# Tokens and attention of a decoder block's first phase turned by VectorE through memory instead of by TensorE

## The chip, the cores and the metric

One core of one Trainium2 chip. The time of a kernel is the device time of one launch in microseconds (us), the median of several launches; lower is better.

## The reference

x and the context are 16 sequences of 512 tokens of 512 channels, fp32. Three residual blocks follow each other, each on the layer norm of x:

```python
# block 1: linear attention of 16 heads of 32, and a convolution over 3 tokens
q, k, v = split_heads(x @ Wq.T), split_heads(x @ Wk.T), split_heads(x @ Wv.T)
q, k = elu(q) + 1, elu(k) + 1
att = (q @ sum_n(k v)) / max(q @ sum_n(k), 1e-6)
x = x + (att + conv3(x)) @ Wp.T + bp
# block 2: cross attention on the context, 4 query heads of 128, one key and value head, rotary, masked softmax
# block 3: a recurrence over the 16 sequences, then a head
f, i, g = sigmoid(x @ wf.T + c @ uf.T + bf), sigmoid(...), tanh(...)
c = f * c + i * g
x = x + tanh(x @ wo.T + c_final @ uo.T + bo)
```

## The kernel before

Four phases a, b, c and d run behind each other in one program, with a queue per engine; an item is one sequence (512 tokens as T=4 tiles of 128, 512 channels as C=4 chunks of 128). Every fp32 matrix is split into a high and a low part (fp32r), and a product is three matmuls (high by high, low by high, high by low; `product`, L130 to L132). ScalarE (ACT) copies the high part, VectorE (DVE) subtracts it for the low part.

Phase a (`phase_a`) is a pipeline of two stages over B=16 items. Step s works on item new=s (keys, values, queries, the state k v) and on old=s-1 (attention, output projection). The order on TensorE (PE) in a step is written out by hand in `step` under `tensor`: four times `attend(t)` of old (L861) and the key product of new, then four value products with `turn_att(c)` (L870) behind each, four query products, the k v sums (L927), the turning of the next item's tokens with `turn_x` (L363; three chunks, the fourth inside the output), and four tiles of the output projection of old. A product is 12 matmuls of 512 columns. `turn_x` and `turn_att` are TensorE transposes of 128x128 blocks by the identity into PSUM, four for each chunk: the products need tokens and attention with the channels on the partitions, and layer norm and attention leave them with the tokens there.

DVE in a step (`vector`): the division of the attention in six groups (`attend`, L702 to L709), `elu_back` of the keys (L695), the norm of the next item (statistics L333, the scale by a power on GpSimd (POOL) L351, `norm_apply` L357), then `z_sum` = turned attention plus convolution (L762) and its low part (L756), `elu_back` of the queries, the mask of k v (L781), the low part of the next tokens (`tokens_low`, L806), the residual (L670) and the two outer taps of the convolution (`outer_taps`, L811, L814). ACT does `elu_front` (L576, L578), the copies of values (L585) and of z's high part (L593), then `tokens_high` (L647) and the middle tap (L652). POOL adds the bias to the residual rows (L555). The DMA queue of SyncE (SP) stores the result of old to DRAM (L534), loads x of new+1 (L456) and the residual rows of old (L516).

The PSUM banks go round: `first` (5 banks) holds the key, value, query, k v products and turned tokens, `second` (3 banks) the attention, turned attention and output. `Rota.freed` names the event that a bank waits for.

After the last step of phase a, stage old of item 15 runs together with the first work of phase b (`self.b_turn_memory`, `keys_values`, `a_last_output`, then `turn_x` of phase b). Phase b's `b_normalise` stands on DVE behind `z_sum` and its low parts.

Phase c is the recurrence: 12 gate tiles (24 products) for each item, and 12 products for item 0. Its tokens are already turned by DVE from item 1 on: 16 DMAs (`shuffle`, L376) copy 32-partition quarters between SBUF tiles, so that each quarter of the channels lies on its own 32 partitions; `turn_squares` (L382) then transposes 32x32 squares for a chunk of 512 tokens in one instruction. Item 0 is turned by PE (`c_turn`). The turned tokens are also stored for phase d.

The core of what changes, before:

```python
for c in range(C):                       # values and the turning of the attention, PE
    if new: ...                          # product of tile c into bank V + c
    if old: turn_att(c)
...
dve.wait_ge(attT_ps.sem, attT_ps.upto(old.b, c))
dve.tensor_tensor(z_sum[c % 2][:, :], second.bank(s, TURNED + c)[:, :], local[old.par][:, c, :], ALU.add)
```

## Time and profile before

| what | us |
|---|---|
| median of 3 runs | 3132.19 (3131.71 to 3132.31) |
| the profiled execution's own time | 3132.6 |
| its span | 3130.9 |
| TensorE busy | 3089.7 |
| VectorE busy | 1834.5 |
| ScalarE busy | 1273.0 |
| GpSimd busy | 838.0 |

How to read it: the span is from the first to the last instruction. "Busy" of an engine is the time in which at least one of its instructions runs; matmuls overlap each other, so the distance between two starts, not the duration, is what one costs. An "x4" row merges four instructions that follow each other, and its duration is that of the four. In the order of time a bracket says how long the engine stood idle before the instruction, and what released it. SPq rows are DMA issues; "to landing" is from the issue to the end of the transfer. PEclk is the granted TensorE clock, as a share of 2.4 GHz.

### The profile page before, as it was taken

To read this page: it belongs to the slowest core of one execution; us is meant where nothing else is said; L and a number is where in the kernel's file an instruction comes from. 1 tells how busy PE (TensorE), PEld (TensorE's weight loads), DVE (VectorE), ACT (ScalarE), POOL (GpSimd) and SP (SyncE) were. 2 spreads that over 40 slices of the span, in tenths; PEclk is the share of its full clock that TensorE was granted. 3 is DMA by queue.
4 is the path that set the end of the run, shared out by engine and by line. 5 is a ranking of instruction groups with operands and counts; after the bars stand their busy time and mean duration, and the time that the engine had idled before them with its cause. 6 is when DMAs were issued, how large, how long until landed. Compare 5 with 4: busy or idle time off the path is not lost.

```text
span 3130.9 us, 40897 instructions
## 1 busy us (share of the span) xinstructions
PE 3089.7 (99%) x15588; PEld 2606.5 (83%) x15588; DVE 1834.5 (59%) x3961; ACT 1273.0 (41%) x2415; POOL 838.0 (27%) x699
## 2 busy tenths in 40 slices
PE   8999999999999999999999999999999999999999
PEld 7888888888878888888888877888888888888887
DVE  6667675666587877787788766423323333231355
ACT  4333333333356766666676653211112111121243
POOL 0101010110146666676666650000000000000144
PEclk9999999999999999999999999999999999999999
DMA  3121121212231221221212132211211112110386
GB/s 111 41 69 54 41 81 41 81 41 83 79 104 69 69 70 56 96 70 56 83 68 70 55 121 81 81 41 41 54 54 55 41 41 54 54 45 26 129 288 227
DMA packets 153363, 236.49 MB, mean 76 GB/s; under 512 B 11345, under 2 KB 48209, under 8 KB 153169
## 3 DMA queue, kind: packets, MB, share of 16 engines
...
## 4 chain that ended last, share of the span: by engine, by line
PE 95%; DVE 2%; issue 1%; ACT 1%; DMA 1%; SPq 0%; POOL 0%; DVEq 0%; ACTq 0%
PE c_p L130 11%; PE c_p L131 11%; PE c_p L132 11%; PE a_p L130 6%; PE a_p L132 6%; PE a_p L131 6%; PE b_n L132 5%; PE b_n L130 5%; PE b_n L131 5%; PE b_t L1622 3%; PE d_p L130 2%; PE d_p L131 2%; PE d_p L132 2%; PE a_r L130 2%; PE a_r L132 2%; PE a_p L927 2%
## 5 line engine op out<-in xcount | busy, mean ns | idle before, releaser
L1242 POOL TENSOR_SCALAR b_soft<-b_soft,b_one_in_sum 128x512 f32<-128x512 f32 x256 | 401.2, 1569 | 300.7 <-DVE b_one_in_sum L1425 300.7
L1867 ACT ACTIVATE c_gate<-c_p,c_bias 128x512 f32<-128x512 f32 x180 | 123.9, 690 | 693.1 <-PE c_p L132 693.1
L1903 DVE TENSOR_TENSOR c_gate<-c_gate,c_gate 128x512 f32<-128x512 f32 x64 | 44.2, 691 | 486.2 <-ACT c_gate L1867 486.2
L1444 DVE TENSOR_TENSOR b_p_lo<-b_t,b_p_hi 128x512 fp32r<-128x512 f32 x256 | 175.3, 685 | 159.9 <-ACT b_p_hi L1299 157.2
L1290 ACT ACTIVATE b_soft<-b_soft,b_minus_top 128x512 f32<-128x512 f32 x256 | 185.2, 724 | 180.8 <-DVE b_minus_top L1436 176.2
L351 POOL TENSOR_TENSOR kept_scale<-c_ln_ve,minus_half 128x4 f32<-128x4 f32 x16 | 16.1, 1009 | 879.6 <-DVE c_ln_ve L343 879.6
L576 ACT ACTIVATE a_elu<-a_p 128x512 f32<-128x512 f32 x128 | 76.5, 598 | 353.1 <-PE a_p L132 353.1
L351 POOL TENSOR_TENSOR a_ln_sc<-a_ln_ve,minus_half 128x4 f32<-128x4 f32 x16 | 16.3, 1017 | 694.7 <-DVE a_ln_ve L343 694.7
L1299 ACT ACTIVATE b_p_hi<-b_t 128x512 fp32r<-128x512 f32 x256 | 151.6, 592 | 108.6 <-PE b_t L1622 108.6
L1436 DVE CUSTOM_DVE_ANT_0 b_soft<-b_l,b_mask_row 128x512 f32<-128x512 f32 x256 | 175.3, 685 | 0.0
L1622 PE MATMUL b_t<-ident,b_soft 128*128 128x128 f32 x1024 | 155.3, 274 | 10.4 <-DVE b_p_lo L1444 9.2
L2090 POOL TENSOR_TENSOR d_x<-d_x,d_y 128x512 f32<-128x512 f32 x60 | 79.8, 1332 | 259.1 <-ACT d_y L2107 259.1
L1622 PEld LDWEIGHTS b_t<-ident,b_soft 128*128 128x128 f32 x1024 | 122.5, 141 | 29.6 <-DVE b_p_lo L1444 14.8
L130 PE MATMUL b_l<-b_k_hi,b_q_hi 128*128 128x512 f32 x256 | 122.7, 479 | 0.0
L695 DVE SCALAR_TENSOR_TENSOR a_q<-a_p,a_elu 128x512 f32<-128x512 f32 x64 | 44.2, 691 | 131.8 <-ACT a_elu L578 131.8
L1905 DVE TENSOR_TENSOR c_gate<-c_gate,c_c_f 128x512 f32<-128x512 f32 x64 | 44.3, 692 | 119.7 <-ACT c_gate L1867 119.7
L130 PE MATMUL c_p<-c_nT_hi,c_wi_hi 128*128 128x512 f32 x256 | 100.9, 394 | 5.3 <-ACT c_gate L1867 5.3
L130 PE MATMUL a_p<-a_Wk_hi,a_xT_hi 128*128 128x512 f32 x256 | 105.3, 411 | 0.2 <-DVE a_Wk_lo L194 0.2
L555 POOL TENSOR_TENSOR a_res<-a_res,a_bp 128x512 f32<-128x512 f32 x64 | 89.6, 1430 | 59.0 <-DMA a_res<-in_x 59.0
L130 PE MATMUL a_p<-a_Wv_hi,a_xT_hi 128*128 128x512 f32 x256 | 104.1, 407 | 0.0
L130 PE MATMUL a_r<-a_Wp_hi,a_z_hi 128*128 128x512 f32 x256 | 102.9, 402 | 0.0
L132 PE MATMUL b_l<-b_k_hi,b_q_lo 128*128 128x512 f32 x256 | 101.5, 397 | 0.0
...
## 6 DMA issues: line engine op xcount, KB each, us to landing
a_res<-in_x SPq DMA_DIRECT2D x16, 1024.0 KB, 5.8
x<-a_res SPq DMA_DIRECT2D x16, 1024.0 KB, 5.2
b_mem<-in_ctx SPq DMA_DIRECT2D x16, 1024.0 KB, 5.4
b_x<-x SPq DMA_DIRECT2D x16, 1024.0 KB, 5.5
b_res<-x SPq DMA_DIRECT2D x16, 1024.0 KB, 5.6
x<-b_res SPq DMA_DIRECT2D x16, 1024.0 KB, 4.4
c_x<-x SPq DMA_DIRECT2D x16, 1024.0 KB, 5.5
d_x<-x SPq DMA_DIRECT2D x16, 1024.0 KB, 5.6
```

Source lines behind the costliest of these rows:

```text
L130: pe.matmul(out, stationary.high, moving.high, start=first, stop=False)
L131: pe.matmul(out, stationary.high, moving.low, start=False, stop=False)
L132: return pe.matmul(out, stationary.low, moving.high, start=False, stop=last)
L555: pool.tensor_tensor(res[:, t, :], res[:, t, :], bp[:, :], ALU.add).then_inc(res_bp.sem, res_bp.unit)
L1242: pool.tensor_scalar(soft[:, at, :], soft[:, at, :], one_in_sum[:, at:at + 1], None, ALU.mult).then_inc(p_norm.sem, p_norm.unit)
L1290: act.activation(soft[:, at, :], soft[:, at, :], ACT.Exp, bias=minus_top[:, at:at + 1], scale=-1.0, accum_out=row_sum[:, at:at + 1]).then_ ...
L1299: act.activation(p[h % 2].high[:, :, t * P:(t + 1) * P], pT_bank[:, :].rearrange("p (i s) -> p i s", i=T), ACT.Copy).then_inc(p_hi.sem, p_ ...
L1436: dve.tensor_tensor_reduce(out=soft[:, at, :], in0=logit_banks[j % 2][:, :], in1=mask_row[b % 2][:, :], scale=-1.0, scalar=3e38, op0=ALU.a ...
L1444: dve.tensor_tensor(part.low, pT_bank[:, :].rearrange("p (i s) -> p i s", i=T), part.high_f32(), ALU.subtract).then_inc(p_lo.sem, p_lo.unit)
L1622: mm = pe.transpose(pT_bank[:, i * P:(i + 1) * P], soft[:, tile(old.b, j), i * P:(i + 1) * P], self.ident[:, :])
L1867: act.activation(gate[j % 2][i][:, :], gating.banks[(3 * j + i) % 6][:, :], ACT.Tanh if g == "c" else ACT.Sigmoid, bias=added[:, i, j:j + ...
L2090: pool.tensor_tensor(x[old.par][:, t, :], x[old.par][:, t, :], y[:, t % 2, :], ALU.add).then_inc(out_sb.sem, out_sb.unit)
```

## The change

Phase a: PE turns only item 0's tokens. For every later item the normed tokens are stored to DRAM (`self.out`, which is overwritten at the end), loaded back by four DMAs (`load_shuffled`) so that channel quarter q lies on partitions 32q to 32q+31, and turned by four DVE transposes (`turn_squares`) into an SBUF tile `turned_f`. The attention goes the same way, through `self.x2`, in two stores and four loads (`shuffle_att`), and four DVE transposes into `z_sum`. Turned this way, partition p of chunk c holds channel 4p+c; so the weights of phase a are turned with `spread` for all four, the convolution's parameters are loaded in that order, and item 0 uses `turn_interleaved`. Readers of the turned tokens (high part, middle tap, low part, outer taps) now read SBUF. On SP the new work stands behind the residual load, first the attention of old, then the tokens of new+1; phase b's first loads move behind it in the last step, and its output weight one step later. POOL's bias additions wait until the next item's tokens are normed. Some tiles move to other addresses.

Phase c: item 1 is turned by PE too (`c_turn` at the gate tiles 8 and 9 of item 0), with ACT copying the turned chunk out of PSUM; the DVE turning of later items moves from the start of a step to behind the second gate column.

The diff, its core (parameters, order and memory lines with no more in them than said above are left out):

```diff
@@ -376,6 +376,12 @@
+    def load_shuffled(self, sp, to, dram, b, event):
+        for q in range(4):
+            sp.dma_start(to[32 * q:32 * (q + 1), :, :].rearrange("m t (r n) -> m (t r) n", n=P),
+                         dram[b, :, q * P:(q + 1) * P].rearrange("(a m) n -> m a n", m=32)).then_inc(event.sem, event.unit)
@@ -430,9 +436,13 @@
+x_shuffled = sb("x_shuffled", [P, T, D])
+turned_f = Place(nc, self.base + 1024 * 196).tile("a_turned_f", [P, C, S])
+att_shuffled = Place(nc, self.base + 1024 * 184).tile("a_att_shuffled", [P, T, D])
...
+self.place = Place(nc, self.base + 1024 * 166)
@@ -440,20 +450,42 @@
+            shuffled, squared = ev("shuffled", 4, 16), ev("squared", C)
+            x_out, att_out = ev("x_out", 1, 16), ev("att_out", 2, 16)
...
-            att_ps, rden_sb, att_sb, attT_ps = ev("att_ps", GROUPS), ev("rden_sb", 2 * GROUPS), ev("att_sb", GROUPS), ev("attT_ps", C)
+            att_ps, rden_sb, att_sb = ev("att_ps", GROUPS), ev("rden_sb", 2 * GROUPS), ev("att_sb", GROUPS)
+            att_moved, attT = ev("att_moved", 4, 16), ev("attT", C)
...
+                if b == 1:
+                    sp.wait_ge(xT_ps.sem, xT_ps.upto(0))
+                if b >= 2:
+                    sp.wait_ge(x_out.sem, x_out.upto(b - 2))
+                sp.dma_start(x[:, :, :], self.token_rows(io["x"], b)).then_inc(N.loaded.sem, N.loaded.unit)
+            def shuffle(sp, b):
+                sp.wait_ge(N.normed.sem, N.normed.upto(b))
+                sp.dma_start(self.token_rows(self.out, b), x[:, :, :]).then_inc(x_out.sem, x_out.unit)
+                sp.wait_ge(x_out.sem, x_out.upto(b - 1))
+                if b >= 2:
+                    sp.wait_ge(squared.sem, squared.upto(b - 2))
+                self.load_shuffled(sp, x_shuffled, self.out, b, shuffled)
+            def shuffle_att(sp, b):
+                for i, (group, tiles) in enumerate(((3, slice(0, 3)), (GROUPS - 1, slice(3, T)))):
+                    sp.wait_ge(att_sb.sem, att_sb.upto(b, group))
+                    sp.dma_start(self.token_rows(self.x2, b)[:, tiles, :], att[:, tiles, :]).then_inc(att_out.sem, att_out.unit)
+                sp.wait_ge(att_out.sem, att_out.upto(b))
                 if b >= 1:
-                    sp.wait_ge(xT_ps.sem, xT_ps.upto(b - 1))
-                sp.dma_start(x[:, :, :], self.token_rows(io["x"], b)).then_inc(N.loaded.sem, N.loaded.unit)
+                    sp.wait_ge(attT.sem, attT.upto(b - 1))
+                self.load_shuffled(sp, att_shuffled, self.x2, b, att_moved)
@@ -490,16 +522,17 @@
-raw = Loader(nc, ctx, "aw", [(io[f"L0_attn_{n}"], w[n]) for n in ("Wk", "Wv", "Wq", "Wp")], (k, res, local[1], raw_p), C, self.ident, 3)
+raw = Loader(nc, ctx, "aw", [(io[f"L0_attn_{n}"], w[n]) for n in ("Wk", "Wv", "Wq", "Wp")], (k, res, local[1], raw_p), C, self.ident, 3, spread=(0, 1, 2, 3))
...
-             + [(kv_sb, g, 0) for g in range(2)] + [(tap2, c, -1) for c in range(C)], B)
-K, V, Q, KV, TURN = 0, T, 2 * T, 2 * T + C, 2 + 2 * T + C
+             + [(kv_sb, g, 0) for g in range(2)], B)
+K, V, Q, KV = 0, T, 2 * T, 2 * T + C
+start_bank = lambda c: first.banks[c + 1]
...
-              [(att_sb, g, 1) for g in range(GROUPS)] + [(z_f, c, 1) for c in range(C)] + [(x1_sb, t, 1) for t in range(T)], B)
-ATT, TURNED, OUT = 0, GROUPS, GROUPS + C
+              [(att_sb, g, 1) for g in range(GROUPS)] + [(x1_sb, t, 1) for t in range(T)], B)
+ATT, OUT = 0, GROUPS
@@ -514,12 +547,17 @@
-if new and new.b == B - 2:
+if old:
+    shuffle_att(sp, old.b)
+if following(new, B):
+    shuffle(sp, new.b + 1)
+if new and new.b == B - 1:
+    sp.wait_ge(shuffled.sem, shuffled.upto(B - 2))
+    self.b_load_mem(sp, 0)
+    sp.wait_ge(tap2.sem, tap2.upto(B - 1))
+    self.b_load_scale(sp)
+    sp.wait_ge(squared.sem, squared.upto(B - 2))
     self.b_load_output_weight(sp)
-if new and new.b == B - 1:
-    sp.wait_ge(xT_ps.sem, xT_ps.upto(B - 1))
-    self.b_load_mem(sp, 0)
-    self.b_load_scale(sp)
@@ -550,6 +588,8 @@
+if following(new, B):
+    pool.wait_ge(N.normed.sem, N.normed.upto(new.b + 1))
@@ -641,15 +681,18 @@
-act.wait_ge(xT_ps.sem, xT_ps.upto(b, c))
+if b == 0:
+    act.wait_ge(xT_ps.sem, xT_ps.upto(0, c))
+else:
+    act.wait_ge(squared.sem, squared.upto(b - 1, c))
...
-act.activation(xT.high[:, c, :], first.bank(b - 1, TURN + c)[:, :], ACT.Copy).then_inc(xT_hi.sem, xT_hi.unit)
+act.activation(xT.high[:, c, :], turned(b, c), ACT.Copy).then_inc(xT_hi.sem, xT_hi.unit)
...
-if b < 2:
+if b == 0:
     act.wait_ge(xT_lo.sem, xT_lo.upto(b, c))
-act.activation(local[b % 2][:, c, :], first.bank(b - 1, TURN + c)[:, :], ACT.Identity,
+act.activation(local[b % 2][:, c, :], turned(b, c), ACT.Identity,
@@ -664,6 +707,9 @@
+def turned(b, c):
+    return start_bank(c)[:, :] if b == 0 else turned_f[:, c, :]
@@ -754,12 +800,15 @@
+dve.wait_ge(att_moved.sem, att_moved.upto(old.b))
 for c in range(C):
-    dve.wait_ge(attT_ps.sem, attT_ps.upto(old.b, c))
-    dve.wait_ge(tap2.sem, tap2.upto(old.b, c))
...
-    dve.tensor_tensor(z_sum[c % 2][:, :], second.bank(s, TURNED + c)[:, :], local[old.par][:, c, :], ALU.add).then_inc(z_f.sem, z_f.unit)
+    squares = att_shuffled[:, :, :].rearrange("p t (n c) -> p c (t n)", c=C)[:, c]
+    dve.transpose(z_sum[c % 2][:, :], squares).then_inc(attT.sem, attT.unit)
+    dve.wait_ge(attT.sem, attT.upto(old.b, c))
+    dve.wait_ge(tap2.sem, tap2.upto(old.b, c))
+    dve.tensor_tensor(z_sum[c % 2][:, :], z_sum[c % 2][:, :], local[old.par][:, c, :], ALU.add).then_inc(z_f.sem, z_f.unit)
@@ -767,6 +816,10 @@
+if after and c == 2:
+    dve.wait_ge(shuffled.sem, shuffled.upto(after - 1))
+    for i in range(C):
+        self.turn_squares(dve, turned_f, x_shuffled, i).then_inc(squared.sem, squared.unit)
@@ -801,17 +854,16 @@
-copied = xT_hi if b < 2 else tap1
-dve.wait_ge(copied.sem, copied.upto(b, c))
-dve.tensor_tensor(xT.low[:, c, :], first.bank(b - 1, TURN + c)[:, :], xT[:, c, :].high_f32(), ALU.subtract).then_inc(xT_lo.sem, xT_lo.unit)
+dve.wait_ge(xT_hi.sem, xT_hi.upto(b, c))
+dve.tensor_tensor(xT.low[:, c, :], turned(b, c), xT[:, c, :].high_f32(), ALU.subtract).then_inc(xT_lo.sem, xT_lo.unit)
...
-bank, loc = first.bank(b - 1, TURN + c), local[b % 2]
-dve.scalar_tensor_tensor(out=loc[:, c, 1:S], in0=bank[:, 0:S - 1], scalar=conv_w[:, c, 0:1],
+row, loc = turned(b, c), local[b % 2]
+dve.scalar_tensor_tensor(out=loc[:, c, 1:S], in0=row[:, 0:S - 1], scalar=conv_w[:, c, 0:1],
...
-dve.scalar_tensor_tensor(out=loc[:, c, 0:S - 1], in0=bank[:, 1:S], scalar=conv_w[:, c, 2:3],
+dve.scalar_tensor_tensor(out=loc[:, c, 0:S - 1], in0=row[:, 1:S], scalar=conv_w[:, c, 2:3],
@@ -881,6 +926,8 @@
+if s == 0 and t >= 1:
+    pe.wait_ge(tap2.sem, tap2.upto(0, t - 1))
@@ -927,28 +974,21 @@
-                    if following(new, B):
-                        for c in range(C - 1 if old else C):
-                            turn_x(new.b + 1, c)
...
-                            if following(new, B) and t == 0:
-                                turn_x(new.b + 1, C - 1)
-
-                def turn_x(b, c):
+                def first_turn(c):
                     if c == 0:
-                        pe.wait_ge(N.normed.sem, N.normed.upto(b))
-                    if freed := first.freed(b - 1, TURN + c):
-                        pe.wait_ge(*freed)
-                    self.turn(pe, first.bank(b - 1, TURN + c), x, c).then_inc(xT_ps.sem, xT_ps.unit)
+                        pe.wait_ge(N.normed.sem, N.normed.upto(0))
+                    self.turn_interleaved(pe, start_bank(c), x, c).then_inc(xT_ps.sem, xT_ps.unit)
...
-                turn_x(0, 0)
-                turn_x(0, 1)
+                first_turn(0)
+                first_turn(1)
                 raw.turn(pe, WK, C - 1, raw_bank(WK, C - 1))
-                turn_x(0, 2)
-                turn_x(0, 3)
+                first_turn(2)
+                first_turn(3)
@@ -1763,15 +1804,15 @@
-if b == 1:
-    sp.wait_ge(xT_ps.sem, xT_ps.upto(0))
-if b >= 2:
-    sp.wait_ge(shuffled.sem, shuffled.upto(b - 2))
+if b <= 2:
+    sp.wait_ge(xT_ps.sem, xT_ps.upto(b - 1))
+else:
+    sp.wait_ge(shuffled.sem, shuffled.upto(b - 3))
...
-if b == 1:
+if b == 2:
@@ -1783,10 +1824,13 @@
-        dve.wait_ge(shuffled.sem, shuffled.upto(b - 1))
-        if b >= 2:
-            dve.wait_ge(turned_stored.sem, turned_stored.upto(b - 2))
+        dve.wait_ge(shuffled.sem, shuffled.upto(b - 2))
+        dve.wait_ge(turned_stored.sem, turned_stored.upto(b - 2))
...
+def second_turned(act, c):
+    act.wait_ge(xT_ps.sem, xT_ps.upto(1, c))
+    act.activation(turned_f[:, c, :], turning.bank(c)[:, :], ACT.Copy).then_inc(squared.sem, squared.unit)
@@ -1816,7 +1860,7 @@
-if following(new, B):
+if following(new, B) and old:
@@ -1846,9 +1890,6 @@
-if new and new.b >= 2:
-    for c in range(C):
-        tokens_high(act, new.b, c)
@@ -1860,6 +1901,10 @@
+if old.b == 0 and j == 3 and i < 2:
+    for c in range(2 * i, 2 * i + 2):
+        second_turned(act, c)
+        tokens_high(act, 1, c)
@@ -1868,9 +1913,9 @@
-if old.b == 0 and j == 0:
+if new and new.b >= 2 and j == 1:
     for c in range(C):
-        tokens_high(act, 1, c)
+        tokens_high(act, new.b, c)
@@ -1891,12 +1936,6 @@
-if new and new.b >= 2:
-    for c in range(C):
-        tokens_turned(dve, new.b, c)
-    for c in range(C):
-        tokens_low(dve, new.b, c)
@@ -1917,13 +1956,7 @@
-if old.b == 0:
-    for c in range(C):
-        tokens_turned(dve, 1, c)
 update(0)
-if old.b == 0:
-    for c in range(C):
-        tokens_low(dve, 1, c)
@@ -1931,7 +1964,12 @@
-if following(new, B):
+    if new and new.b >= 2:
+        for c in range(C):
+            tokens_turned(dve, new.b, c)
+        for c in range(C):
+            tokens_low(dve, new.b, c)
+if following(new, B) and not (old and old.b == 0):
@@ -1945,9 +1983,14 @@
+    if old.b == 0 and j == 3:
+        for c in range(C):
+            tokens_low(dve, 1, c)
...
+if old.b == 0:
+    norm(dve, 2)
@@ -1970,6 +2013,9 @@
+if old.b == 0 and 8 <= n <= 9:
+    self.c_turn(pe, 1, 2 * (n - 8))
+    self.c_turn(pe, 1, 2 * (n - 8) + 1)
```

## Rows read from the trace of the kernel before

**Rows 1.** The page: PE's busy time, and the chain that ended last by engine
```profile
PE 3089.7 (99%) x15588; PEld 2606.5 (83%) x15588; DVE 1834.5 (59%) x3961; ACT 1273.0 (41%) x2415; POOL 838.0 (27%) x699
...
PE 95%; DVE 2%; issue 1%; ACT 1%; DMA 1%; SPq 0%; POOL 0%; DVEq 0%; ACTq 0%
```

**Rows 2.** Busy time of each engine in a stretch: PE, PEld, DVE, ACT, POOL, clock, DMA
```profile
390.00:445.00 55.00, 55.00 (x294) 47.01 (x293) 36.39 (x68) 19.27 (x32) 6.57 (x5) 1.00 0.17 58
```

**Rows 3.** PE in order of time, one step of phase a (start us, us)
```profile
390.01 1.06 PE L861 MATMUL a_r<-a_kv,a_q 128*128 128x132 f32 x8
...
407.26 0.60 PE L870 MATMUL a_r<-ident,a_att 128*128 128x128 f32 x4
407.62 0.47 PE L130 MATMUL a_p<-a_Wv_hi,a_xT_hi 128*128 128x512 f32 x1
407.93 0.39 PE L131 MATMUL a_p<-a_Wv_lo,a_xT_hi 128*128 128x512 f32 x1
408.15 0.39 PE L132 MATMUL a_p<-a_Wv_hi,a_xT_lo 128*128 128x512 f32 x1
...
431.79 1.47 PE L363 MATMUL a_p<-ident,a_x 128*128 128x128 f32 x12
433.01 0.48 PE L130 MATMUL a_r<-a_Wp_hi,a_z_hi 128*128 128x512 f32 x1
...
444.51 1.06 PE L861 MATMUL a_r<-a_kv,a_q 128*128 128x132 f32 x8
```

**Rows 4.** DVE in order of time, the same step
```profile
404.34 0.29 DVE L709 TENSOR_TENSOR a_att<-a_r,a_rden 128x128 f32<-128x128 f32 x1
...
407.58 5.80 DVE L357 TENSOR_SCALAR a_x<-a_x,a_ln_mv,a_ln_sc 128x512 f32<-128x512 f32 x4 [0.54 <-POOL a_ln_sc L351]
...
439.94 0.74 DVE L811 SCALAR_TENSOR_TENSOR a_local<-a_p,a_conv_w,a_local 128x511 f32<-128x511 f32 x1
...
442.67 0.74 DVE L811 SCALAR_TENSOR_TENSOR a_local<-a_p,a_conv_w,a_local 128x511 f32<-128x511 f32 x1
```

**Rows 5.** DVE in order of time, step 0 and phase c: norm alone, four transposes
```profile
35.87 1.91 DVE L357 TENSOR_SCALAR a_x<-a_x,a_ln_mv,a_ln_sc 128x512 f32<-128x512 f32 x4
...
1938.67 4.01 DVE L382 STREAM_TRANSPOSE c_turned_f<-c_x_shuffled 128x512 f32<-128x512 f32 x4 [11.91 <-DMA c_x_shuffled<-c_x]
```

**Rows 6.** SP in order of time: 1024 KB, then 4 of 256 KB; 16 of 64 KB
```profile
853.09 0.37 SPq L1028 DMA_DIRECT2D b_x<-x  x1
854.19 2.29 SPq L1084 DMA_DIRECT2D b_raw_qw<-in_L_xattn_q_w  x4
...
1926.79 10.39 SPq L376 DMA_DIRECT2D c_x_shuffled<-c_x  x16
```

**Rows 7.** The four b_raw_qw DMAs, issue to landing
```profile
DMA to landing us min/median/max: 5.5/6.2/6.7
```

**Rows 8.** DMA issues by line: count, KB each, median us to landing
```profile
a_res<-in_x SPq DMA_DIRECT2D x16, 1024.0 KB, 5.8
...
out<-d_x SPq DMA_DIRECT2D x4, 256.0 KB, 2.0
```

**Rows 9.** From phase a to b in order of time: PE, DVE, SP
```profile
884.03 0.37 SPq L516 DMA_DIRECT2D a_res<-in_x  x1
...
888.45 0.36 PE L130 MATMUL b_n<-b_kvw_hi,b_nT_hi 128*128 128x256 f32 x1
...
894.84 2.88 DVE L357 TENSOR_SCALAR b_x<-b_x,b_ln_mv,b_n_scale 128x512 f32<-128x512 f32 x4
...
897.87 0.63 PE L363 MATMUL b_n<-ident,b_x 128*128 128x128 f32 x4 [0.68 <-DVE b_x L357]
```

**Rows 10.** PE in order of time in phase c, item 0
```profile
1943.97 0.80 PE L130 MATMUL c_p<-c_nT_hi,c_wi_hi 128*128 128x512 f32 x1 [5.30 <-ACT c_gate L1867]
...
1949.23 0.39 PE L130 MATMUL c_p<-c_nT_hi,c_wc_hi 128*128 128x512 f32 x1
```

**Rows 11.** Busy time of each engine in a stretch of phase c; clock before DMA share
```profile
1944.00:1946.00 2.00, 2.00 (x5) 1.61 (x6) 2.00 (x4) 1.32 (x3) 0.00 (x0) 0.50 1.03 387
```

More of the change, by code:

```diff
@@ L418, in phase_a @@
             q = sb("q", [P, C, S])
-            att = sb("att", [P, BLOCKS, P])
+            att = sb("att", [P, T, D])
             raw_p = Place(nc, self.place.offset).tile("a_raw_p", [P, C, D])
@@ L463, in first_loads @@
                 with nc.allow_non_contiguous_dma(reason="small parameters, once"):
[L464 to L465 removed]
+                    sp.dma_start(conv_w[:, :, :], io["L0_attn_conv_w"].rearrange("(p c) k -> p c k", p=P)).then_inc(params.sem, params.unit)
+                    sp.dma_start(conv_b[:, :], io["L0_attn_conv_b"].rearrange("(p c) -> p c", p=P)).then_inc(params.sem, params.unit)
                     sp.dma_start(bp[:, :], io["L0_attn_bp"].rearrange("(a n) -> a n", a=1).to_broadcast([P, D])).then_inc(params.sem, params.unit)
@@ L705, in attend @@
                         if g == 0 and old.b >= 1:
-                            dve.wait_ge(attT_ps.sem, attT_ps.upto(old.b - 1))
+                            dve.wait_ge(att_out.sem, att_out.upto(old.b - 1))
                         dve.wait_ge(rden_sb.sem, rden_sb.upto(old.b, 2 * g + 1))
                         heads = lambda ap: ap.rearrange("p i (h e) -> p i h e", h=HC)
-                        dve.tensor_tensor(heads(att[:, blocks, :]), heads(bank[:, :, 0:P]),
+                        dve.tensor_tensor(heads(att[:, :, :].rearrange("p t (c n) -> p (t c) n", c=C)[:, blocks, :]), heads(bank[:, :, 0:P]),
                                           rden[:, blocks, :].unsqueeze(3).broadcast_to([P, n, HC, HD]), ALU.mult).then_inc(att_sb.sem, att_sb.unit)
@@ L863, in attend @@
                                 mm.then_inc(att_ps.sem, att_ps.unit)
-                    def turn_att(c):
-                        if freed := second.freed(s, TURNED + c):
-                            pe.wait_ge(*freed)
-                        pe.wait_ge(att_sb.sem, att_sb.upto(old.b))
-                        for t in range(T):
-                            mm = pe.transpose(second.bank(s, TURNED + c)[:, t * P:(t + 1) * P], att[:, t * C + c, :], self.ident[:, :])
-                        mm.then_inc(attT_ps.sem, attT_ps.unit)
                     if new is None:
@@ L897, in step @@
                                 pe.wait_ge(*freed)
+                            if s == 0 and t == 0:
+                                pe.wait_ge(tap2.sem, tap2.upto(0, C - 1))
                             bank = first.bank(s, V + t)
@@ L903, in step @@
                                 turn_weight(WP, 2 * t)
-                        if old:
-                            turn_att(c)
                     if new:
@@ L984, in phase_b @@
             k_f = sb("k_f", [P, T, HD])
-            mask_u8 = [sb(f"mask_u8{i}", [P, S], U8) for i in range(2)]
+            mask_place = Place(nc, self.base + 1024 * 196)
+            mask_u8 = [mask_place.tile(f"b_mask_u8{i}", [P, S], U8) for i in range(2)]
             mask_row = [sb(f"mask_row{i}", [P, S]) for i in range(2)]
@@ L996, in phase_b @@
             raw_qw, raw_kvw = sb("raw_qw", [P, C, H * HD]), sb("raw_kvw", [P, C, 2 * HD])
-            raw_ow = Place(nc, self.base + 1024 * 160).tile("b_raw_ow", [P, H, D])
+            raw_ow = Place(nc, self.base + 1024 * 158).tile("b_raw_ow", [P, H, D])
             params = ev("params", 4, 16)
```

3 lines of the change are left out of this document (removed).

## The prediction

> **What bounds the kernel now.** I read the page first: TensorE (PE) is busy for 99% of the span, and the chain of work that ended last is 95% PE [rows 1]. In a stretch of steady phase a, PE is busy for 55.00 of 55.00 us at full clock, VectorE (DVE) for 36.39, ScalarE for 19.27 [rows 2]. So in phase a only what PE issues counts, until another chain becomes as long. The order of time gives one step as 444.51 - 390.01 = 54.50 us [rows 3]; I count times within a step from its attention start, 390.01 = 0. DVE finishes the last attention group at 404.34 + 0.29, so at 14.6, and begins the next tokens' norm at 407.58 = 17.6 [rows 4].
>
> **What leaves PE.** A turned chunk is four transposes. One between products takes 407.62 - 407.26 = 0.36, and the first matmul behind it 0.31 instead of 0.22 (407.62 to 407.93, against 407.93 to 408.15), 0.45 in all; twelve in a row take 433.01 - 431.79 = 1.22 [rows 3], 1.3 with the slow start. A step has four such singles of attention, and for the tokens the twelve and a single: 5 x 0.45 + 1.3 = 3.55, I take 3.6. Steps 1 to 14 have all of it: 14 x 3.6 = 50.4. Step 15 has only the attention's, 1.8. Step 0 has 16 token transposes, 1.8, of which I count 1.1, because PE then waits for the state's mask, some 0.7 later, which they hid. The first weights and tokens are now read with a stride of four; this I cost at nothing, and at 10% of 80 transposes of 0.11 it would be 0.9.
>
> **What goes to DVE.** Four transposes take 4.01 [rows 5], so eight in a step are 8.0. Against that the norm shrinks: beside POOL's bias additions it takes 5.80 [rows 4], without them 1.91 [rows 5], and now POOL waits for it; -3.9. DVE is then busy for about 40 of 50.9 us, so its sum does not bind; the order of its queue may. POOL's additions start at about 19.5 instead of 17.5 and end near 25, while the residual that reads them comes after 40: covered.
>
> **The two trips through memory** are what can bind. Call D the time from the first issue of four 256 KB loads to the last landing. The nearest row is b_raw_qw, also four of 256 KB in pieces of 512 bytes: issued at 854.19 in 2.29, the last landed at most 6.7 after its issue, near 862.7, but behind 1024 KB issued at 853.09 [rows 6, 7]. Together 9.6 for 2 MB; a lone MB lands after 5.8 [rows 8], so a further one costs 3.8. Alone, with 1.8 between first and last issue, I take D = 7; low end 6. High end: the 16 quarter copies of phase c, first issued at 1926.79 [rows 6] and waited for until 1938.67 [rows 5]: 11.9, most of it issue time of 16 DMAs, while here there are four; so I stay near b_raw_qw. What no row shows is a 1 MB load into 32 partitions at a time.
>
> The Trainium skill (SBUF — State Buffer, Door 1: The DMA port swizzle) speaks against the change here: a transfer to 32 partitions reaches only half of the SBUF ports, measured at 189 GB/s for 1 MiB, and it says that two such transfers serialize. By it a megabyte takes some 5.5 instead of 3.8, D an estimated 8.5, and the sum below would be 1.5 higher; no row here shows it.
>
> Now the chain in a step. Attention is complete at 14.6; its last tile is stored by 16.6 (256 KB: 2.0 [rows 8]); the first three quarters went out earlier, behind the residual load. Landed: 16.6 + 7 = 23.6. DVE waits there from 19.6 on, with the queries' elu_back queued behind it, and with them ScalarE's later elu and PE's second k v sum (needed at 38). Four rounds of transpose, sum and low part, 1.1 + 0.64 + 0.61 each: 9.4, and 0.6 for ScalarE's last copy: 33.6. The output projection reads z from 40 on: slack 6. Then two rounds of elu, 2.5: 36.1. The tokens: normed at 19.5, their store queues behind the attention's loads, 23.6 + 3.8 = 27.4, and with D landed at 34.4: in time. Four transposes: 40.1; two elu_back and two masks, 1.9: 42.0; then low part, residual and two taps, 442.67 - 439.94 = 2.73 for a chunk [rows 4], so the fourth low part is done at 42.0 + 3 x 2.73 + 0.64 = 50.8. The next step begins at 54.5 - 3.6 = 50.9 and first reads that chunk 2.8 later, at 53.7. Slack 2.9. On the tokens' side landing is 20.4 + 2D against 36.1 + 2.9 = 39.0, so nothing shows up to **D = 9.3**; beyond it a step grows by 2 for each us.
>
> **The end of phase a.** Here nothing covers the trip. The residual load is issued at 884.03 [rows 9], lands at 889.8, the attention's store behind it at 893.6, D: 900.6, DVE's four rounds 10.0: 910.6, phase b's first norm (894.84 to 897.72 now; 1.9 to 2.9): 912.5. PE first turns b_x at 897.87 [rows 9]; it would at 912.7: +14.8. Its products that need neither, from 888.45 on [rows 9], are few (48 of 256 columns). So PE idles long. In phase c it idled for 5.30 and the next twelve matmuls then took 1949.23 - 1943.97 = 5.26 instead of 2.7 [rows 10], at granted clock 0.50, the 1.2 GHz level [rows 11]: 2.5 more. Sum +17.3. In step 15 phase b's first loads leave SP some 13 us later; they land near 28 to 38, before their readers at 40, and ScalarE's squares of b_mem in between delay the values by less than their banks' slack: nothing.
>
> **Phase c.** The wait of 5.30 is item 0's gate update standing on DVE behind the turning of item 1, which waits 11.91 for its copies [rows 5, 10]. That goes, with the 2.5 of slow clock; 16 transposes come to PE, 1.8. Late next would be ScalarE's copy of the second pair of chunks, in the shadow of two gate tiles of 2.7 each. -6.0. For later items DVE's turning moves to the middle of a 65 us step in which it is mostly idle: nothing.
>
> **Sum**, against the profiled execution's 3132.6 (0.4 above the median of the runs, 3132.19): -50.4 - 1.8 - 1.1 - 6.0 + 17.3 = -42.0, so 3090.6.
>
> **Rivals.** (1) *The trips outgrow their slack, gain kept in part.* With D = 10 a step is 52.3: -14 x 2.2 - 8.9 + 20.3 = -19.4, 3113. For it: both trips wait on one queue, and D for 32 partitions is unmeasured; against: b_raw_qw. The skill's 8.5 stays short of 9.3. (2) *Slower: the loop DVE, store, load, DVE becomes the step.* Place: PE's first key product waiting for the low part of the next tokens. At D = 11.9 a step is 50.9 + 2 x 2.6 = 56.1: 14 x 1.6 - 8.9 + 22.2 = +35.7, 3168. It turns to a loss from D = 10.7 on. For it: the copies in phase c did take that long; against: their time is 16 issues. (3) *The end costs less*: clock kept, D = 6, and part of the store overlapped: 3084 or below.
>
> **Numbers.** Forecast 0.68, rival 1 0.18, rival 2 0.08, rival 3 0.06. The range takes in D from 5 to 10 and an end between 10 and 20: 3078 to 3116. A measurement of this kernel tells 0.2%, some 6 us, from no change: faster 0.90, within 0.2% 0.02, slower 0.08, the middle being a crossing point between cases.
>
> **What would show it.** Right: steps of 50.9 with no PE wait in steady phase a; DVE idle some 4 before each first attention transpose; one PE idle of 10 or more near 840 to 860, followed by clock 0.5; no 5.3 in phase c. Wrong: PE waiting for a_xT_lo in every step (rival 1 or 2), norm_apply still at 5.8, or an end under 10.

## The result, and the profile after

The changed kernel takes 3089.89 us (median of 4 runs, 3088.35 to 3090.46) against 3132.22 for the kernel before on the same chip: a ratio of 0.9864, with a 95% interval of 0.9847 to 0.9881. The forecast was 3090.6, in a range of 3078 to 3116. The profiled execution took 3088.35 and its span is 3086.6. I give times within a step from its attention start, as the prediction does.

The page of the changed kernel: busy time, the chain, the groups of the two new DVE waits and PE's new one, and two kinds of DMA issue.

```profile
PE 3034.9 (98%) x15108; PEld 2557.7 (83%) x15108; DVE 1894.2 (61%) x4081; ACT 1272.5 (41%) x2419; POOL 828.9 (27%) x699
...
PE 96%; DVE 2%; issue 1%; ACT 1%; DMA 1%; POOL 0%; SPq 0%; DVEq 0%; ACTq 0%
...
L808 DVE STREAM_TRANSPOSE a_z_sum<-a_att_shuffled 128x512 f32<-128x512 f32 x64 | 69.9, 1092 | 90.5 <-DMA a_att_shuffled<-x 89.4
...
L130 PE MATMUL a_r<-a_Wp_hi,a_z_hi 128*128 128x512 f32 x256 | 102.6, 401 | 15.5 <-DVE a_z_lo L802 15.5
...
a_res<-in_x SPq DMA_DIRECT2D x16, 1024.0 KB, 6.8
a_att_shuffled<-x SPq DMA_DIRECT2D x64, 256.0 KB, 5.1
```

Against [rows 1] PE has 480 instructions and 54.8 us of busy time less, and its only new wait of any size is one for `a_z_lo`, 15.5 us in three places. The new idle of 89.4 us on DVE stands in front of the attention's transposes, where PE never waits for it, except once, at the end of phase a. The next fence holds one whole step of phase a, then a stretch behind item 15's trip (the way of its attention through memory and back); columns as in [rows 2], with the granted clock before the DMA share.

```profile
368.07:418.86 50.79, 50.79 (x258) 43.25 (x256) 39.20 (x74) 19.00 (x32) 6.04 (x5) 1.00 0.54 145
852.00:860.00 8.00, 5.68 (x12) 3.48 (x12) 7.77 (x13) 4.08 (x9) 0.00 (x0) 0.50 0.00 0
```

PE is still busy for the whole step, now 50.79 us long instead of 54.50, and DVE for 39.20. Steps 2 to 15 all have this length; step 1 has 52.46 (61.68 to 114.14), where before it had 55.91. The same step in order of time, PE's two ends, then SP, then DVE, against [rows 3, 4]:

```profile
368.07 0.61 PE L913 MATMUL a_r<-a_kv,a_q 128*128 128x132 f32 x4
...
418.86 0.84 PE L913 MATMUL a_r<-a_kv,a_q 128*128 128x132 f32 x6
```
```profile
377.74 5.32 SPq L484 DMA_DIRECT2D x<-a_att  x2
385.56 1.91 SPq L382 DMA_DIRECT2D a_att_shuffled<-x  x4
387.58 0.42 SPq L475 DMA_DIRECT2D out<-a_x  x1
395.49 1.91 SPq L382 DMA_DIRECT2D a_x_shuffled<-out  x4
```
```profile
382.40 0.29 DVE L755 TENSOR_TENSOR a_att<-a_r,a_rden 128x128 f32<-128x128 f32 x1
...
385.64 1.91 DVE L357 TENSOR_SCALAR a_x<-a_x,a_ln_mv,a_ln_sc 128x512 f32<-128x512 f32 x4 [0.54 <-POOL a_ln_sc L351]
...
393.06 1.08 DVE L808 STREAM_TRANSPOSE a_z_sum<-a_att_shuffled 128x512 f32<-128x512 f32 x1 [5.51 <-DMA a_att_shuffled<-x]
...
401.45 1.47 DVE L802 TENSOR_TENSOR a_z_lo<-a_z_sum,a_z_hi 128x512 fp32r<-128x512 f32 x2
403.38 0.69 DVE L741 SCALAR_TENSOR_TENSOR a_q<-a_p,a_elu 128x512 f32<-128x512 f32 x1 [0.46 <-ACT a_elu L618]
404.53 0.69 DVE L741 SCALAR_TENSOR_TENSOR a_q<-a_p,a_elu 128x512 f32<-128x512 f32 x1 [0.46 <-ACT a_elu L618]
405.14 4.15 DVE L388 STREAM_TRANSPOSE a_turned_f<-a_x_shuffled 128x512 f32<-128x512 f32 x4
...
418.99 0.68 DVE L858 TENSOR_TENSOR a_xT_lo<-a_turned_f,a_xT_hi 128x512 fp32r<-128x512 f32 x1
```

Attention is complete at 382.69 = 14.6, its loads are issued from 385.56 = 17.5 (foretold 16.6), the first transpose is at 393.06, so D is 7.50 (foretold 7), the z rounds end at 34.9 (33.6), the tokens' squares at 41.2 (40.1), and their fourth low part at 51.6 (50.8). PE needs that part 2.8 into the next step, at 53.6: a slack (time to spare before anybody waits) of 2.0.

From phase a to b, in order of time SP, then DVE, then PE, against [rows 9]:

```profile
830.47 0.37 SPq L549 DMA_DIRECT2D a_res<-in_x  x1
830.88 1.03 SPq L484 DMA_DIRECT2D x<-a_att  x2
841.14 1.92 SPq L382 DMA_DIRECT2D a_att_shuffled<-x  x4
```
```profile
848.47 1.08 DVE L808 STREAM_TRANSPOSE a_z_sum<-a_att_shuffled 128x512 f32<-128x512 f32 x1 [14.64 <-DMA a_att_shuffled<-x]
...
858.24 1.91 DVE L357 TENSOR_SCALAR b_x<-b_x,b_ln_mv,b_n_scale 128x512 f32<-128x512 f32 x4
```
```profile
852.75 0.77 PE L130 MATMUL a_r<-a_Wp_hi,a_z_hi 128*128 128x512 f32 x1 [13.93 <-DVE a_z_lo L802]
...
860.31 0.67 PE L363 MATMUL b_n<-ident,b_x 128*128 128x128 f32 x4
```

The last attention starts 53.5 us earlier than before (825.15 against 878.68), but b_x is turned 35.2 us behind it instead of 19.2, so that only 37.6 are left at this point. PE idles for 13.93, and what follows runs at a granted clock of 0.50, the 1.2 GHz level.

### The profile page after: what moved, and what is told of

Read it like the earlier page. It is cut to its first block, busy times and chain, and to the rows that moved or that the text cites. A ratio compares the mean times of both kernels' runs of the same rounds, so it can differ in the third digit from the quotient of the medians.

```text
span 3086.6 us, 40196 instructions
## 1 busy us (share of the span) xinstructions
PE 3034.9 (98%) x15108; PEld 2557.7 (83%) x15108; DVE 1894.2 (61%) x4081; ACT 1272.5 (41%) x2419; POOL 828.9 (27%) x699
## 4 chain that ended last, share of the span: by engine, by line
PE 96%; DVE 2%; issue 1%; ACT 1%; DMA 1%; POOL 0%; SPq 0%; DVEq 0%; ACTq 0%
PE c_p L131 11%; PE c_p L132 11%; PE c_p L130 11%; PE a_p L130 6%; PE a_p L132 6%; PE a_p L131 6%; PE b_n L132 5%; PE b_n L130 5%; PE b_n L131 5%; PE b_t L1663 3%; PE d_p L131 2%; PE d_p L130 2%; PE d_p L132 2%; PE a_r L130 2%; PE a_r L131 2%; PE a_r L132 2%
## 5 line engine op out<-in xcount | busy, mean ns | idle before, releaser
L1942 DVE TENSOR_TENSOR c_gate<-c_gate,c_gate 128x512 f32<-128x512 f32 x64 | 44.2, 690 | 503.1 <-ACT c_gate L1912 503.1
L808 DVE STREAM_TRANSPOSE a_z_sum<-a_att_shuffled 128x512 f32<-128x512 f32 x64 | 69.9, 1092 | 90.5 <-DMA a_att_shuffled<-x 89.4
L130 PE MATMUL a_r<-a_Wp_hi,a_z_hi 128*128 128x512 f32 x256 | 102.6, 401 | 15.5 <-DVE a_z_lo L802 15.5
L1944 DVE TENSOR_TENSOR c_gate<-c_gate,c_c_f 128x512 f32<-128x512 f32 x64 | 44.3, 692 | 116.3 <-ACT c_gate L1912 116.3
L633 ACT ACTIVATE a_z_hi<-a_z_sum 128x512 fp32r<-128x512 f32 x64 | 40.5, 633 | 153.0 <-DVE a_z_sum L811 153.0
L595 POOL TENSOR_TENSOR a_res<-a_res,a_bp 128x512 f32<-128x512 f32 x64 | 80.4, 1290 | 82.3 <-DMA a_res<-in_x 53.9
L130 PE MATMUL b_e<-b_p_hi,b_v_hi 128*128 128x512 f32 x256 | 100.5, 393 | 0.7 <-DVE b_enc_lo L1490 0.7
```

Source lines behind the costliest of these rows:

```text
L130: pe.matmul(out, stationary.high, moving.high, start=first, stop=False)
L595: pool.tensor_tensor(res[:, t, :], res[:, t, :], bp[:, :], ALU.add).then_inc(res_bp.sem, res_bp.unit)
```

## The experiments

The kernel before was measured beside each group of experiments and took 3131.8 to 3133.0 each time (medians; the last a single run), so the runs can be compared with one another. "After" names the changed kernel.

### e1: item 15 turned by TensorE

In the last step SyncE sends nothing through memory, and DVE adds `local` to a PSUM bank as before. PE's part of the edit:

```diff
...
                         self.b_turn_memory(pe, C - 1)
+                        for c in range(C):
+                            if c == 0:
+                                pe.wait_ge(att_sb.sem, att_sb.upto(old.b))
+                            if c == C - 1:
+                                pe.wait_ge(z_f.sem, z_f.upto(old.b, 1))
+                            self.turn_interleaved(pe, second.bank(s, OUT + c % 3 + c // 3), att, c).then_inc(last_turned.sem, last_turned.unit)
```

> The changed kernel, but item 15's attention, which has no step of its own to hide a trip in, is turned by TensorE again (with a stride of four) and goes through no memory. My account: the end of phase a is the only place where the trip costs anything, 16.0 us by the two traces (first turn of b_x 35.2 us after the last attention's start instead of 19.2), so all of it comes back, less nothing: 3090 - 16 = 3074 us, within 3; b_x is turned about 19 us after the last attention's start, no PE wait over 3 us between 820 and 860. Rival: the end is held by something else that the change moved as well (phase b's first loads leave SyncE later, behind the shuffles), so that b_x is turned at +30 or later and 3085 us or more remains.

Measured: 3074.27 us (3071.34 to 3075.77), ratio to before 0.9814 (0.98 to 0.9829). PE in order of time:

```profile
830.06 1.73 PE L369 MATMUL a_r<-ident,a_att 128*128 128x128 f32 x12 [0.84 <-DVE a_att L756]
833.65 0.75 PE L369 MATMUL a_r<-ident,a_att 128*128 128x128 f32 x4 [1.85 <-DVE a_z_sum L817]
842.89 0.63 PE L363 MATMUL b_n<-ident,b_x 128*128 128x128 f32 x4
```

The trip of item 15 costs 15.6 us, and it alone: b_x is turned 842.89 - 823.72 = 19.2 behind the last attention's start again, with no PE wait above 1.85. This version beats both kernels.

### e2: the attention of all items turned by TensorE

Edit: e1's turning in every step, one chunk behind each value product as in the kernel before, with a stride of four.

> The changed kernel with the attention of all items turned by TensorE again; the tokens still go through memory. My account: each of 15 steps gets four single turned chunks back, at 0.45 each 1.8 us, +27 us, and the end gives 16 back: 3101 us, steps of 52.7. Rival A: a turned chunk between products costs only its four matmuls' recorded 0.27 each less overlap, 1.1 us per step: +16 - 16, so 3090, steps of 52.0. Rival B: the attention's trip slows something hidden in each step (SyncE, the second load), and a step falls by less than 1.8 for it: 3095.

Measured: 3104.24 (3103.73 to 3105.38), ratio 0.9912 (0.9896 to 0.9929). That is 30.0 above e1 for 15 steps, 2.0 each, where 1.8 was foretold; in its trace a step is 52.84, which is 2.05 above 50.79. The stride is 0.17 of it: in the kernel before, step 15, which turned the attention alone and without a stride, took 52.67, so 1.88 above. The group of these transposes agrees: with a stride they take 285 ns (median) instead of 272 to 273, and there are 16 in a step.

```profile
L369 PE MATMUL a_r<-ident,a_att x256: 270/285/385, 80.5 to 865.7; 128*128 128x128 f32 x128
```

So rivals A and B fall: the turned chunk costs its matmuls and the slow start of the product behind it.

### e3: POOL does not wait for the norm

```diff
-                        if following(new, B):
-                            pool.wait_ge(N.normed.sem, N.normed.upto(new.b + 1))
                         pool.wait_ge(res_in.sem, res_in.upto(old.b))
```

> The changed kernel without POOL's wait for the norm: its bias additions run beside norm_apply again. My account: norm_apply goes from 1.91 back to about 5.8, the store and load of the tokens queue behind the attention's anyway, and VectorE's idle before the first attention transpose falls from 5.5 to about 1.6: no effect, 3090 us within 2, steps of 50.9. Rival: the tokens land 3.9 later, more than the 2.9 us of slack of their fourth low part: +1 us in each of 14 steps, 3104 us, with a PE wait for a_xT_lo in every step.

Measured: 3090.35 (3089.04 to 3090.78). DVE's groups in a step (380 to 432):

```profile
L357 DVE TENSOR_SCALAR a_x<-a_x,a_ln_mv,a_ln_sc 128x512 f32<-128x512 f32 x4 | 5.8, 1512 | 0.5 <-POOL a_ln_sc L351 0.5
L806 DVE STREAM_TRANSPOSE a_z_sum<-a_att_shuffled 128x512 f32<-128x512 f32 x4 | 4.4, 1093 | 0.7 <-DMA a_att_shuffled<-x 0.6
```

The norm takes 5.8 again and the idle before the attention's transpose falls from 5.5 to 0.6. The shorter norm that the change brings is worth nothing in these steps: it only turns work into waiting.

### e4: phase c's part alone

Edit: the kernel before, with phase c of the changed one.

> The kernel before, with the change's phase c alone (item 1 turned by TensorE, the later items' turning moved inside the step); phases a, b and d as before. My account: the wait of 5.3 us and the slow-clock stretch behind it go, 16 transposes come: -6, so 3126 us. Rival: VectorE's moved work delays gate updates in the later steps, or ScalarE's two copies take the wait's place; then -2 or less, 3130 us or more.

Measured: 3126.29 (3125.22 to 3127.15, 10 runs), ratio 0.998 (0.9971 to 0.9989): -6.1. PE's waits behind 1700 us no longer hold the 5.3 for c_gate of [rows 10], and nothing took its place: the largest left is the one that phase b has in both kernels.

```profile
PE b_t L1622 <- DVE b_p_lo L1444: 6.6, 8, 1.5
PE b_n L185 <- DVE c_wf_lo L194: 1.3, 1, 1.3
```

### e5 and e6: the loads in 8 and in 16 copies, on e1

```diff
         for q in range(4):
-            sp.dma_start(to[32 * q:32 * (q + 1), :, :].rearrange("m t (r n) -> m (t r) n", n=P),
-                         dram[b, :, q * P:(q + 1) * P].rearrange("(a m) n -> m a n", m=32)).then_inc(event.sem, event.unit)
+            for t in range(0, 4, 1):
+                sp.dma_start(to[32 * q:32 * (q + 1), t:t + 1, :].rearrange("m t (r n) -> m (t r) n", n=P),
+                             dram[b, t * P:(t + 1) * P, q * P:(q + 1) * P].rearrange("(a m) n -> m a n", m=32)).then_inc(event.sem, event.unit)
```

That is the core of e6 (the counts of the events change with it); e5 has steps of two.

> e1 (item 15 turned by TensorE, 3074), but each shuffled load of 1 MB goes out as eight copies of 128 KB to 32 partitions instead of four of 256 KB. That lengthens both trips by the issue time of four more copies, about 0.48 each: the attention's D from 7.5 to about 9.4, the tokens' by as much and started 1.9 later. By the recorded threshold (nothing up to D = 9.3, then 2 us a step per us) there is no or hardly any loss: 3074 to 3077. By the slack as the trace of after has it (fourth low part of the tokens 1.1 before it is needed, not 2.9) the step is longer by about 0.7: 14 x 0.7 = +10, 3084. Rival: the trips are not near the path at all; 3074 and no PE wait for a_xT_lo.

> The same with sixteen copies of 64 KB for each shuffled load (each to 32 partitions, pieces of 512 bytes as before). Issue alone is 16 x 0.48 = 7.6 or more, D some 12. My model of the loop (slope 2 from D = 9.3): a step is 5.4 longer, 14 x 5.4 = +76, 3150, with a PE wait for a_xT_lo of over 4 in every step. By the trace's own times it is +7 a step, 3172. Rival: work of other engines absorbs it, the loss is under 30 us.

Measured: e5 3073.0 (3071.56 to 3074.44), e6 3090.68 (3089.33 to 3093.61). Eight copies change nothing beyond the spread, since D did not grow: 392.63 - 385.30 = 7.33. The issue time, 3.77 us instead of 1.91, was covered by the transfers. Sixteen do make the trip longer (SP and DVE, then PE's waits from 60 to 830):

```profile
392.82 7.45 SPq L383 DMA_DIRECT2D a_att_shuffled<-x  x16
```
```profile
402.03 1.09 DVE L815 STREAM_TRANSPOSE a_z_sum<-a_att_shuffled 128x512 f32<-128x512 f32 x1 [8.88 <-DMA a_att_shuffled<-x]
```
```profile
PE a_p L987 <- DVE a_q L743: 7.5, 7, 1.9
PE a_r L920 <- DVE a_res L718: 4.3, 6, 0.9
```

D is 9.21, not 12, and the loads start 392.82 - 388.28 = 4.5 behind the end of attention instead of 2.9: the trip is 3.4 longer in all. A step lost 16.4 / 14 = 1.2 on average. So about 2.2 us of slack were used up first, if each us beyond it costs one. PE never waited for a_xT_lo, which all my theories named. It waited for two other readers behind the same DVE queue: the bank that the queries' first elu frees for the second k v sum, and the bank that the last residual frees for the next attention. In after, that elu ends at 404.07, and PE's k v products start at 404.37 and come to their second half 1.96 later (as long as the first half takes in e6), at 406.3: 2.3 of slack by the trace, close to e6's 2.2. The two waits hold 11.8 of the 19.6 us by which this execution's steps are longer than those of after (steps of 50.79 to 54.75 us); part of the rest is a stretch at a lower granted clock (0.97 over the step at 268.13), the remainder I have not traced. My figures for e6 (+76, or +98) were wrong because D was 9.2, not 12, and because a cost of about 1 us for each us comes ahead of that of 2.

### e7 and e11: sixteen copies to 128 partitions, on e1

e7 sends one block of 32 token rows to the four quadrants in a copy; e11 has the same copies with 128 rows of one column block as source. The core of e7's edit (the four copies that it replaces are left out):

```diff
+        for t in range(4):
+            for r in range(4):
+                a = 4 * t + r
+                sp.dma_start(to[:, t, r * P:(r + 1) * P],
+                             dram[b, 32 * a:32 * (a + 1), :].rearrange("m (q n) -> q m n", n=P)).then_inc(event.sem, event.unit)
```

> As e6, sixteen copies of 64 KB in pieces of 512 bytes, but each copy writes all 128 partitions (one block of 32 token rows, its four quarters to the four quadrants) instead of 32 partitions. Same number of issues, same bytes, same pieces. If the number of partitions doesn't matter, the time and the first-issue-to-last-landing are those of e6 within 10%, since issue time sets them. If copies to 32 partitions are held to half of the ports (the Trainium skill, SBUF - State Buffer, Door 1), e7's landing after issue is shorter than e6's by a third or more and the program is faster than e6 by over 20 us.

> e7's slow copies again: sixteen of 64 KB, each to all 128 partitions in pieces of 512 bytes, but the source is 128 rows of one column block, so one run of 128 rows in place of e7's four runs (quarters) of 32 rows. Other squares arrive than the transposes want, so the turned values are not the real ones; count, size, pieces and partitions are e7's. In e7 such copies kept the DMA engines busy at a share of 0.24, the same in every slice, as four of sixteen engines would. If the four-fold outer run of the source confines a copy to four engines, the share rises here to e6's 0.42 or more, D falls from 14.8 to 9 or less, and the time to 3090 or below. If copies of 128 partitions by themselves cost more to issue or to move, it stays near 3259.

Measured: e7 3258.85 (3253.02 to 3261.18), ratio to before 1.0399 (1.0381 to 1.0416); e11 3090.13, one run. The issue stretches of e7 and of e11, one fence each, columns as above:

```profile
400.24:410.94 10.70, 10.70 (x49) 8.87 (x48) 1.50 (x4) 0.67 (x2) 5.03 (x4) 1.00 0.24 72
```
```profile
392.44:399.84 7.40, 7.40 (x34) 6.14 (x33) 0.48 (x2) 0.60 (x1) 5.04 (x4) 1.00 0.41 119
```

In e7 the share is 0.24, about 4 of 16 DMA engines, and the issue itself is held up (10.70 instead of 7.46). With a source of one run it is 0.41, and D falls from 414.99 - 400.24 = 14.75 to 401.60 - 392.44 = 9.2, that of e6, by DVE's first attention transpose in e7 and in e11:

```profile
414.99 1.09 DVE L816 STREAM_TRANSPOSE a_z_sum<-a_att_shuffled 128x512 f32<-128x512 f32 x1 [13.25 <-DMA a_att_shuffled<-x]
```
```profile
401.60 1.08 DVE L815 STREAM_TRANSPOSE a_z_sum<-a_att_shuffled 128x512 f32<-128x512 f32 x1 [8.68 <-DMA a_att_shuffled<-x]
```

So neither of e7's two theories holds: the source's pattern decided. The Trainium skill (DMA: Bandwidth & Descriptors, Why a DMA increments its semaphore by 16 and not by 1) states the rule: a copy uses the largest number of engines up to 16 that divides the slowest dimension of both of its patterns, here four. I had not applied it to my own edit; the trace agrees with it.

e7 does test the loop. All 15 steps of its phase a are longer, (3258.85 - 3074.27) / 15 = 12.3 each. Against e6, D grew from 9.1 to 15.1 (means over 15 steps) and the step by (3258.85 - 3090.68) / 15 = 11.2: 1.9 us for each us of D. DVE now also waits for the tokens in every step, 5.97 us at 433.16. This is the loop of rivals 1 and 2 with a slope near their 2. It exists; the change simply stays below it. Two things differ from what the rivals said. PE does not wait for a_xT_lo here either, but for a bank of the output (a_res, 46.4 us in all), for ScalarE's values (40.9) and for the queries' elu (26.5), all queued behind the loads. And the chain that ended last holds, beside both trips, the load of the next tokens (a_x<-in_x, 8.3 us at 448.62), which no rival named. The granted clock is 0.94 over these steps, so a part of the growth may be the clock's, though that chain holds little of PE (SyncE's issues of the loads alone are 30.9% of it); I have not separated it.

### e8 and e9: partitions or pieces

Both on the changed kernel and with four copies of 256 KB: e8 to all 128 partitions in pieces of 512 bytes, e9 to 32 partitions in pieces of 2048.

```diff
+            sp.dma_start(to[:, q, :].rearrange("p (r n) -> p r n", n=P),
+                         dram[b, :, q * P:(q + 1) * P].rearrange("(r p) n -> p r n", p=P)).then_inc(event.sem, event.unit)
```

> The changed kernel, its shuffled loads still four copies of 256 KB in pieces of 512 bytes, but each writes one tile of all 128 partitions instead of all tiles of 32 partitions. It fetches other squares than the transposes want, so the turned tokens and attention are not the real ones; work, sizes and order are the same. In after such a load moves 175 to 190 GB/s with the DMA engines busy throughout, while whole tiles (pieces of 2 KB, 128 partitions) move at 382. If the 32 partitions do it (the Trainium skill, SBUF - State Buffer, Door 1), the rate is near 380 here, a load lands some 2.5 us sooner (D 5 instead of 7.5), and the end of phase a is 2.5 shorter. If the pieces of 512 bytes do it, rate and D stay, 3089.

> The counterpart: four copies of 256 KB, each to 32 partitions, in pieces of 2048 bytes (whole rows of the tile, not shuffled, so again the turned values are not the real ones). If the 32 partitions do it: 175 to 190 GB/s and D 7.5 as in after. If the pieces do it: near 380 GB/s, D about 5, the end of phase a 2.5 shorter, 3086.

Measured, one run each: 3088.6 and 3089.93, which says nothing beside a spread of 2. The rates say more. A load of the tokens with nothing beside it (behind the gap; ahead of the gap stands the end of the tokens' store), slices of 0.25 us, busy tenths of the DMA engines over GB/s: the changed kernel (394 to 404 us), e8 (392 to 402), e9 (394 to 404).

```profile
DMA  9994000000578999999999999999995000000000
GB/s 410 410 369 156 0 0 0 0 0 18 154 221 254 313 307 277 184 180 172 174 174 227 233 213 176 178 174 182 174 127 72 8 0 0 0 0 0 0 0 0
```
```profile
DMA  2111000000679879999999994211000000000000
GB/s 90 74 74 66 0 0 0 0 0 20 184 229 317 262 182 297 319 330 303 311 277 287 301 275 131 78 43 31 16 0 0 0 0 0 0 0 0 0 0 0
```
```profile
DMA  9999300000196797999899989989682100000000
GB/s 410 418 410 352 123 0 0 0 0 0 33 139 115 279 393 254 279 205 205 156 246 238 262 180 238 254 148 246 115 148 41 25 0 0 0 0 0 0 0 0
```

The engines are busy for nearly all of the load in all three. To 32 partitions they settle at 172 to 233 GB/s with pieces of 512 bytes and at about 150 to 280 with pieces of 2048; to 128 partitions with pieces of 512 bytes at about 300. So it is the 32 partitions, for the larger part, and the pieces beside them. D for item 15's attention is 848.47 - 841.14 = 7.33 in after, 6.17 in e8 and 6.90 in e9, and over all 16 attentions its mean is 7.4, 6.5 and 6.9. e8 gained 1.0 to 1.2 in D, less than half of what I gave it. The rule of the Trainium skill that the prediction weighed (SBUF — State Buffer, Door 1: The DMA port swizzle), half of the ports for 32 partitions, agrees with these rows; by its rate I had put D at 8.5, by rows of before at 7, and it was 7.5.

### e10: item 15's trip ahead of the residual's load

```diff
+                    if old and new is None:
+                        shuffle_att(sp, old.b)
```

ahead of the residual's load in SyncE's step, and the later call only where there is a `new`.

> The changed kernel, but in the last step SyncE issues the attention's store and shuffled load ahead of the residual's load instead of behind it. My account of the end: the store then has no megabyte in front of it, so it lands at least 3.8 us sooner (1 MB at the rate of a whole tile), and also needn't wait for the store of the step before; b_x is turned 4 to 6 us sooner, 3090 - 5 = 3085. Rival: the trip of item 15 is held by its own latency and the attention's end, so 1 us or less, 3089 or more.

Measured: 3085.55 (3085.16 to 3086.49), ratio 0.9851 (0.9834 to 0.9867): 4.3 less than after. The loads are issued at 834.27 instead of 841.14, 6.9 sooner, but b_x is turned at 856.92, only 3.4 sooner. D is 0.5 longer (842.14 - 834.27 = 7.87), and 2.9 was given back on DVE, whose rounds take 12.7 instead of 9.8:

```profile
844.99 1.50 DVE L813 TENSOR_TENSOR a_z_sum<-a_z_sum,a_local 128x512 f32<-128x512 f32 x1
846.42 1.75 DVE L804 TENSOR_TENSOR a_z_lo<-a_z_sum,a_z_hi 128x512 fp32r<-128x512 f32 x1
```
```profile
844.68 5.86 POOL L597 TENSOR_TENSOR a_res<-a_res,a_bp 128x512 f32<-128x512 f32 x4 [23.73 <-DMA a_res<-in_x]
```

The two DVE operations take 0.69 in after, where POOL is idle. The residual's later arrival moved POOL's additions, which had been done while DVE waited, onto DVE's rounds.

## Why the prediction was right, point by point

Each term against the two traces, in us:

| term | foretold | measured | from |
| --- | --- | --- | --- |
| steps 1 to 15 | -52.2 | -53.6 | last attention less the first: 825.15 - 61.68 against 878.68 - 61.60 |
| step 0 | -1.1 | +0.1 | 61.68 against 61.60 |
| end of phase a | +17.3 | +16.0 | b_x turned at +35.2 against +19.2; e1: +15.6 |
| phase b | 0 | -0.9 | 1861.77 against 1900.23 at c_x's first turn, less the 37.6 |
| phase c | -6.0 | -5.8 | the rest of the span's 44.3; e4: -6.1 |
| sum | -42.0 | -44.2 | spans 3130.9 and 3086.6; medians -42.3 |

The trace shows 2 us more than the medians because the profiled execution of the changed kernel is the shortest of its four (1.5 below its median) and that of the kernel before is 0.4 above its median.

The mechanism of the gain and of the one loss was right. That the sum met the medians within 0.7 us is in part luck: in the trace three terms came out lower by 0.9 to 1.4 (the steps, the end, phase b) and step 0 higher by 1.2, so that the sum was off by 2, and the choice of execution took that back.

*The steps.* A step was foretold at 50.9 and is 50.79, PE's work alone: from 100 to 800 us PE waits for nothing. What leaves a step is thus 3.71, not 3.6, and 1.88 in step 15, not 1.8: a turned chunk was costed slightly too low, which makes 1.4 over all steps. (763.47 / 15 is 50.90 only because step 1 is longer.) e2 gives the attention's share as 2.05 a step where TensorE reads it with a stride.

*The trip.* D was 7.5 against 7, from b_raw_qw and the lone megabyte [rows 6 to 8], and 2.0 of slack were left where 2.9 were foretold. What was off is the reader: "nothing shows up to D = 9.3" rested on the tokens' low part. In e6 the queries' elu and the last residual came first, with a slope of 1. The chain did name the second k v sum, "needed at 38", but I did not carry that bound on to the threshold. Had the loads not also started later behind the attention's end, e6's loss would have set in at D = 7.5 + 2.2 = 9.7, so the number 9.3 nearly held though its reason did not: that is luck.

*The end.* The store's landing behind the residual load (9.6 foretold and 10.7 measured from the load's issue to the shuffled loads'), D, DVE's rounds of 10.0 (9.8) and the shorter norm of b_x are all there; they come to 16.0 where 14.8 was foretold. The 2.5 for the slow clock is not there, so two errors partly cancel in the +17.3. PE ran at the lower level from 852 to 860 while it still waited for z_lo twice (0.76 and 0.81), and it came to b_x at 860.31, only 0.16 behind the end of b_x's norm (858.24 + 1.91), so that the slow stretch lay almost wholly in the shadow of DVE's chain. In phase c the slow stretch stood on PE's own path, and there its 2.5 counted.

*Phase b.* The -0.9 was not aimed at. It arises in the first 100 us behind b_x's turn: from 40 to 60 us behind it the granted clock is 0.72 and then 0.94 in the kernel before, 0.83 and then 1.00 in the changed one.

*Step 0.* Its -1.1 nearly came: from the k v products to the first attention it takes 61.68 - 57.30 = 4.38 instead of 61.60 - 56.26 = 5.34, so -0.96, with the wait for the state's mask (a_kv) 0.6 against 0.7. But the k v products themselves begin 1.04 later. 0.35 of it is the first turn, which starts at 11.65 instead of 11.30. The other 0.7 is the stride: 48 transposes of weights take 285 ns (median) instead of 272, and the distance from one group of eight to the next, with the product between them, is 3.73 to 3.74 instead of 3.61 to 3.63, six times. The kernel before, then the changed one:

```profile
20.94 1.03 PE L185 MATMUL a_r<-ident,a_res 128*128 128x128 f32 x8
...
24.55 1.04 PE L185 MATMUL a_r<-ident,a_res 128*128 128x128 f32 x8
```
```profile
21.31 1.12 PE L185 MATMUL a_r<-ident,a_res 128*128 128x128 f32 x8
...
25.04 1.12 PE L185 MATMUL a_r<-ident,a_res 128*128 128x128 f32 x8
```

So "this I cost at nothing" was wrong, its bound of 0.9 was not.

*POOL's wait.* The norm went to 1.91 as foretold; e3 shows that the steps needed none of it.

*Rivals.* Rivals 1 and 2 had the right loop at the wrong distance, and named the wrong wait: e7 shows the loop with a slope of 1.9, but at a D of 15.1, twice that of the change, and in neither e6 nor e7 does PE wait for a_xT_lo. Rival 3 did not happen as it is; e10 shows that 4.3 of the end could be had by order alone, and e1 that 15.6 could.
